# Identity products ahead of TensorE's waits, and 45 instead of 32 convolution groups read from the on-chip table

## The reference

```
x = layernorm(x + edge_network(x))      # mean over incoming edges of a 4-layer MLP of (x_i, x_j - x_i)
x = layernorm(x + conv1(x))             # sum of neighbours, degree-normalised on both sides
x = layernorm(x + conv2(x))             # the same with out- and in-degree, a 32x32 weight, relu
x = layernorm(x + gat(x))               # 3 GATv2 layers: 8 heads of 32, softmax over incoming edges,
                                        #   mean over heads, batch norm
```

## Time and profile before

| | before |
|---|---|
| median of 3 timed runs | 6000.18 us (5997.96 to 6010.52) |
| the profiled execution, first to last instruction | 7770.9 us |
| TensorE products busy in it | 5760.6 us (74%), 43965 instructions |
| VectorE busy | 3565.2 us (46%) |
| ScalarE busy | 1748.7 us (23%) |
| GpSimd busy | 4059.1 us (52%) |
| mean granted clock of TensorE | 0.821 |

### The profile page before, as it was taken

The page is one execution under the profiler, slowest core; times in us unless marked ns, Lnnn a source line. Parts: engine busy times, 40 slices in busy tenths (PEclk is TensorE's granted clock), DMA queues, the critical chain, the costliest instruction groups (busy, mean ns, idle before and its releaser), DMA issues.

```text
span 7770.9 us, 130521 instructions
## 1 busy us (share of the span) xinstructions
PE 5760.6 (74%) x43965; PEld 3691.2 (48%) x43965; DVE 3565.2 (46%) x6811; ACT 1748.7 (23%) x3748; POOL 4059.1 (52%) x4236
## 2 busy tenths in 40 slices
PE   5888886566646666578887876877787758788777
PEld 4666665455545454334444443444444424444444
DVE  5444444455544444444444444444444534444446
ACT  2222222344420000022222221222222122222221
POOL 4555554666646566455555533555555245555551
PEclk8888887777767776688888897888888878888988
DMA  4444443222212222233333332333333223333332
GB/s 103 129 129 129 128 128 98 51 56 56 56 47 56 55 56 55 49 82 93 88 91 88 89 85 56 90 90 89 92 89 89 80 58 92 89 89 93 91 88 65
DMA packets 688913, 648.23 MB, mean 83 GB/s; under 512 B 401396, under 2 KB 483771, under 8 KB 688251
## 3 DMA queue, kind: packets, MB, share of 16 engines
q1 hardware_dynamic: 548266, 463.96, 20.0%
q0 software_dynamic: 135616, 175.22, 11.8%
q10 hardware_dynamic: 4368, 0.70, 0.1%
HBM read 550.21 MB, written 89.17 MB: 82 GB/s over the span
## 4 chain that ended last, share of the span: by engine, by line
PE 43%; issue 22%; another core or an unknown queue 21%; DVE 9%; ACT 3%; DVEq 2%; DMA 0%; POOL 0%; ACTq 0%; POOLq 0%
PE ps L1055 14%; PE ps L900 7%; PE ps L994 5%; PE ps L1005 2%; PE ps L1015 2%; PE ps L855 2%; PE ps L915 1%; PE ps L980 1%; DVE region L1778 1%; DVE acc L1803 1%; PE ps L974 1%; PE ps L864 1%; ACT region L662 1%; PE ps L811 1%
## 5 line engine op out<-in xcount | busy, mean ns | idle before, releaser
L381 POOL DMA_INDIRECT rows<-table,idx x2340 | 2258.3, 965 | 2221.5 <-ACT region L651 1042.6
L1055 PE MATMUL ps<-region,hot 128*128 128x272 f32 x4992 | 1528.3, 457 | 295.8 <-DVE region L1756 159.4
L1055 PEld LDWEIGHTS ps<-region,hot 128*128 128x128 f32 x4992 | 1040.8, 219 | 690.9 <-issue 461.8
L1803 DVE TENSOR_TENSOR acc<-acc,ps 128x272 f32 x1248 | 544.5, 436 | 1685.6 <-remote 808.6
L662 ACT ACTIVATE region<-ps 128x512 f32<-128x512 f32 x1248 | 677.3, 595 | 2691.7 <-remote 1438.8
L900 PE MATMUL ps<-hot,region 128*128 128x192 bf16 (+1 forms) x6144 | 896.1, 309 | 444.2 <-issue 429.0
L900 PEld LDWEIGHTS ps<-hot,region 128*128 128x128 bf16 x6144 | 703.4, 123 | 590.9 <-issue 529.9
L368 POOL DMA_INDIRECT rows<-table,idx x728 | 696.6, 957 | 534.2 <-PE ps L835 320.4
L994 PE MATMUL ps<-xT,wcat 64*128 64x512 f32 x2496 | 771.8, 696 | 170.4 <-issue 92.1
L1778 DVE TENSOR_TENSOR region<-ps,region 128x1056 f32<-128x1056 f32 x582 | 724.7, 1251 | 44.0 <-issue 40.4
L398 POOL DMA_INDIRECT rows<-table,idx x576 | 546.6, 949 | 378.5 <-issue 157.3
(11 more groups left out here) (304 smaller groups left out, 6646.9 us busy)
## 6 DMA issues: line engine op xcount, KB each, us to landing
hot<-hot_dram SPq DMA_DIRECT2D x624, 256.0 KB
turned<-turned_dram SPq DMA_DIRECT2D x624, 128.0 KB
rows<-table,idx POOLq DMA_INDIRECT x3644
hot_dram<-hot SPq DMA_DIRECT2D x104, 512.0 KB
xwin<-table SPq DMA_DIRECT2D x1664, 24.0 KB
region<-hot_dram SPq DMA_DIRECT2D x64, 512.0 KB
region<-d_dram SPq DMA_DIRECT2D x104, 256.0 KB
turned_dram<-turned SPq DMA_DIRECT2D x104, 256.0 KB
```

The lines of the kernel that those rows point to most:

```text
L381: pool.indirect_dma_start(rows[:, n % 2, j, :], None, table, bass.IndirectOffsetOnAxis(ap=idx[:, s:s + 1], axis=0)).then_inc(rows_in3[n % ...
L1055: mm = pe.matmul(ps[:, sum_bank(k, side, i), 0:PC + H], hot[:, b, 4 * side + 2 * i + j, :], px[b][:, 4 * side + 2 * i + j, :], start=(j == ...
L1803: v.tensor_tensor(at, at, ps[:, sum_bank(k, side, i), 0:PC + H], ALU.add).then_inc(att_added, 1)
```

## The change

`DENSE` takes 45 of the 104 groups instead of 32, so `PLAIN` has 59 instead of 72. TensorE gets products whose results nobody reads: `keep_warm` multiplies the 128 x 128 bf16 identity by itself, four copies wide (512 columns), into a bank that is written anew afterwards; `keep_warm_beside` does so with 448 columns into the columns of the degree bank that hold no counts.

```diff
-DENSE = [g for g in range(G) if 7 * g % 16 >= 11]
-PLAIN = [g for g in range(G) if 7 * g % 16 < 11]
+DENSE = [g for g in range(G) if 7 * g % 16 >= 9]
+PLAIN = [g for g in range(G) if 7 * g % 16 < 9]
...
+        full_moving = identb[:, :].unsqueeze(1).broadcast_to([P, 4, P])
+        part_moving = identb[:, 0:112].unsqueeze(1).broadcast_to([P, 4, 112])
+        def keep_warm(pe, bank, times):
+            for _ in range(times):
+                pe.matmul(ps[:, bank, :], identb[:, :], full_moving, start=True, stop=True, skip_group_check=True)
+        def keep_warm_beside(pe, bank, times):
+            for _ in range(times):
+                pe.matmul(ps[:, bank, 64:512], identb[:, :], part_moving, start=False, stop=False, skip_group_check=True)
...  pe_pass0, in each step
                     first_layer(s - 1)
+                    keep_warm(pe, 0, 1)
...
                 if s < G:
+                    if s > 0:
+                        keep_warm(pe, 0, 2)
                     rows_in(s)
...  pe_convolution, in each dense item
                     read(i)
+                    keep_warm_beside(pe, DEG, 1)
                     if i > 0:
                         sum_dense(i - 1)
+                    keep_warm_beside(pe, DEG, 1)
...  pe_attention, in each step u
                     z_half(u, 0)
+                    keep_warm(pe, XT, 1)
                 if phase == 1 and ends:
+                    if u < G:
+                        keep_warm(pe, XT, 4)
                     pe.wait_ge(carry_made, at + 1)
...
                 if phase == 2 and ends and done > 0:
+                    if u < G:
+                        keep_warm(pe, XT, 2)
                     pe.wait_ge(fdiag_made, at + 1)
...
                 if u + 1 < G:
+                    keep_warm(pe, XT, 2)
                     rows_in(u + 1)
```

## The result

The changed kernel takes 5894.51 us (median of 4 runs, 5893.74 to 5895.43) against 5999.07 us of the kernel before, timed beside it: ratio 0.9839, 95% interval 0.9816 to 0.9863, 105 us faster. The forecast was 38 us faster. The signs of its terms were right, and one size was not.

The account below looks back on a forecast made before the run. GpSimd's gathers and the time between their stretches (5896 us) were taken to bound the kernel, with TensorE also full in the attention. 6000 - 190 (convolutions) + 152 (attention) + 0 (edge network) = 5962 us; range 5780 to 6200.

Parts of the forecast that it names:

- What bounds the kernel: Whole kernel: 4220 GpSimd gathers at 1.25 us, 5275 us, plus 621 us outside the stretches; attention fills TensorE as well.
- the floor: Whole kernel: gathers plus the time outside their stretches, 5896 us, with the timed median only 104 us above it.
- the holes: TensorE idle with nothing to wait for in the 7770.9 us profile, taken as the profiler's own and left out.
- Edge network, 0: Edge network: 310 dummies hidden behind GpSimd's gathers, cost 0; up to 69 us if that cover is gone.
- Attention, +152: Attention: loop dummies stream 208 us over three layers, idle time takes 56; chunk-end ones (45 us) count as nothing.
- 0.5 us leaves +52: Attention, lower bound: with 0.5 us of TensorE idle time a piece, the dummies cost only 52 us.
- Convolution, -190: Two convolutions: 13 groups moved from gathers to table reads, passes of 640 and 620 us, 1260 instead of 1450.
- the low bound: Convolutions: 590 us for each of the two passes, a gain of 270 us.
- the allowance: Convolutions: time added for waits among GpSimd, TensorE and VectorE, whose needs were taken as nearly the same.
- The clock as the gain: Rival, attention: dummies holding 2.4 GHz give back up to 420 us, total 5640, or 5850 at half effect; chance 0.10.
- the dummies would not hold the clock there: Rival, convolutions: items cost twice 3.1 us, +780 us at worst, total 6900; chance 0.05.
- The attention in full: Rival, attention: loop dummies cost 208 to 253 us, convolutions give back only 80 to 150, total 6120; chance 0.38.

Follow-up runs that it names:

- the second profile: The kernel before the change, unedited, profiled once more: one run of 5986.93 us, profiled span 5985.2 us.
- run 9: Changed kernel with dummies in the two convolutions alone, those of the attention and edge network removed: 5737.96 us, ratio 0.9588 to the kernel before.
- run 4: Changed kernel without the attention's dummies; edge network, convolutions and 45 groups as changed: 5738.24 us, ratio 0.9568 to the kernel before.
- run 2: Kernel before with 45 dense groups instead of 32 and no dummies at all: 5765.06 us, ratio 0.9615.

## Why the prediction was wrong in size

*What bounds the kernel.* Right in kind: the gathers and what lies between them, and the convolutions are bound by gathers alone, before as after. The 621 us between the stretches came from the 7770.9 us execution, though. In the second profile they are 559 us (52.7, 60.2, 31.4, 35.0, 126.4, 126.7 and 126.3), so the floor was 5275 + 559 = 5834 us, not 5896. The kernel lay 151 us above it, 115 of them in the attention (3040 for 2925 us of gathers) and 31 in the edge network (941 for 910). That the 7770.9 us of the earlier trace rows were no picture of the timed runs was right too: profiled again, the kernel spans 5985.2 us. How the holes arose there was not tried.

*Edge network, 0.* Right: 941.4 and 940.3 us, and run 9. GpSimd's waits for TensorE there come to 20 us before and after.

*Attention, +152.* Right by 151 us between the two profiles and 156 between run 4 and the changed kernel, and by parts: the chunk-end dummies, counted at nothing, cost 13 us alone, not clear of noise, and the loop's, counted at 152, 44 + 114 = 158 alone. But the size of the idle time behind it was wrong, and the number came out partly by luck. The forecast spread 0.2 us of idle time over each piece, from a need of 9.5 to 9.7 us on TensorE. Measured, TensorE needs 17.78 / 2 = 8.89 us a piece away from chunk ends and is idle for 1016.5 - 919.65 = 97 us a layer, 0.93 us a piece. By the forecast's own reckoning, in which 0.5 us leaves +52, that much would have hidden the dummies wholly. It did not, because most of it sits in few places. TensorE's waits in the first layer of the kernel before, second profile:

```profile
PE ps L980 <- DMA rows<-table,idx: 42.8, 14, 16.8
PE ps L1055 <- DVE region L1756: 28.6, 11, 3.0
PE ps L1055 <- issue: 14.3, 11, 1.7
PE ps L1055 <- DVE acc L1803: 7.4, 11, 0.7
```

The layer's first row reads wait 16.8 us, and the aggregations (line 1055) wait 50 us, 11 times for each cause, behind the ends of chunks. Of these 50 us the changed kernel still has 26 in its first layer. Between chunk ends TensorE had only the 1 us in two pieces by which it was ahead of GpSimd, and six dummies there take 1.42. The section "Part 3: Packing small matmuls" of the Trainium skill's page "TensorE: Matmul & The Clock Gate" says that products never overtake each other. The starts at 2706.21 and 2706.44 agree with the rule. Paid in full, the dummies would have cost 253 us; they cost 156, and the other 97 us of the streaming in three layers fell into idle time.

*Convolution, -190: the step that failed.* The forecast found gathers 590, TensorE 590 to 630 and VectorE 560 to 600 us a pass, and from "three engines then need nearly the same, so none hides another's waits" it took 640 and 620. Measured are 597.5 and 598.1, the low bound. Two things in it were wrong. First, the needs of TensorE and VectorE. The timeline of the second convolution after shows the item by its starts:

```profile
1904.91 0.35 PE L812 MATMUL ps<-identb 128*128 128x448 bf16 x1
1905.10 2.22 PE L916 MATMUL ps<-hot,region 128*128 128x224 bf16 x24
1907.16 0.35 PE L812 MATMUL ps<-identb 128*128 128x448 bf16 x1
1907.35 0.53 PE L931 MATMUL ps<-region 128*128 128x32 f32 x4
1907.71 0.35 PE L812 MATMUL ps<-identb 128*128 128x448 bf16 x1
1907.90 0.50 PE L943 MATMUL ps<-rows,region 128*128 128x96 bf16 x8
1908.24 2.22 PE L916 MATMUL ps<-hot,region 128*128 128x224 bf16 x24
```

From 1904.91 to 1907.71 an item is 2.80 us, not 3.1 (reading 2.06 where 2.25 was taken, summing 0.36 for 0.44), and a plain group, 1907.90 to 1908.24, is 0.34, not 0.55. The 2.25 and 0.44 were taken from start to start too, but in the 7770.9 us execution. In the earlier trace rows the product behind the reading starts 0.02 us after the reading's recorded end (2658.51 + 2.23, then 2660.76), here 0.16 us before it (1905.10 + 2.22, then 1907.16). In the second profile of the kernel before the reading is 2.06 us as well:

```profile
2001.35 2.22 PE L900 MATMUL ps<-hot,region 128*128 128x224 bf16 x24
2003.41 0.56 PE L915 MATMUL ps<-region 128*128 128x32 f32 x4
```

So the rows of the forecast held about 0.2 us an item in which no product started. The 0.55 was scaled from a recorded duration (0.42 us for six products), whose modelled end overlaps what follows. So TensorE needs 180 x 2.80 + 59 x 0.34 = 524 us, and with the 40 us of degree counts 564 in the first pass. VectorE's item in the same stretch:

```profile
1899.46 1.21 DVE L1681 TENSOR_TENSOR region<-dloc,ps 128x1024 bf16<-128x1024 f32 x1
...
1902.40 0.48 DVE L1654 TENSOR_SCALAR region<-region,lanes 128x1024 bf16<-128x1024 f16 x1
...
1904.45 0.48 DVE L1654 TENSOR_SCALAR region<-region,lanes 128x1024 bf16<-128x1024 f16 x1
```

2.05 us an item; with 2.94 us a plain group (1899.46 to 1902.40) it is 180 x 2.05 + 59 x 2.94 = 542, and 579 with the counts. Both lie 2 to 11% under the gathers' 590. Second, the waits that TensorE and VectorE have for each other cost nothing as long as GpSimd is the slowest: no gather of these stretches waits beyond its own pace once the table is stored, with dummies or without (run 2), even in the first pass, where VectorE is within 2% of it. At 51 groups the same sums give, for the second pass, TensorE 589 and VectorE 574 us against 530 of gathers. There the two that hand each item to and fro are the slowest, and the allowance is seen: 606.6 us and a tail 34 us longer, 641, 9% over the larger need.

*The rivals.* The clock as the gain is ruled out: before, the attention's granted clock was 0.97 outside that one execution, and the kernel is faster without its dummies. The convolution's clock did rise, from 0.80 to 1.00 and 0.99, but the stretch is set by GpSimd: run 2 reaches the same stretches at 0.94 and 0.97. The section "Why this matters for your kernels" of that page of the Trainium skill bids keep the array busy so that its clock does not drop. The rise agrees. That the dummies would not hold the clock there did not happen. The attention in full (up to 253 us) is ruled out by 156.

Put together: 6000 - 249 + 151 + 0 = 5902 us against 5894.5 measured. What of the 59 us between -190 and -249 belongs to the mis-sized needs and what to the allowance can't be parted, since both went into one number.

## What to carry to other kernels

Take an engine's need per item from start to start of a repeated pattern that runs without idle time, in an execution as long as the timed runs, and not from recorded durations; and add an allowance for waits among engines only where those that hand work to and fro are themselves the slowest. Work that is moved from the slowest engine to others is worth the slowest engine's saving until they cross it, and a run to either side finds the crossing (39, 45 and 51 groups: 5844, 5738 and 5839 us). Products that only keep TensorE busy cost nothing that shows where another engine set the pace (the edge network and the convolutions here), and most of their streaming, 156 of 253 us, where TensorE was nearly full: without the attention's, the same kernel takes 5738 us.

## What the runs showed beside

One profiled execution can be 30% longer than the timed runs, with the surplus spread over TensorE as idle time that nothing released (7770.9 us, and 5985.2 for the same kernel profiled again). A profile whose span doesn't fit the timed runs is to be taken again before its waits are read.

TensorE's clock fell in stages that did not care: 0.80 over the convolutions before, 0.90 with 39 groups, with each gather on time in both. And in a queue that seems full the place of an idle product still matters: 0.18 us ahead of the row reads, 0.14 behind the first z, and at the ends of chunks no cost that is clear of noise (13 us for 210).
